# Six banks for the first row maxima, and the expert biases fetched tile by tile: one change in a two-layer attention and mixture-of-experts kernel

## What is computed

```python
h = jax.nn.silu(xs @ Wg[e] + bg[e]) * (xs @ W1[e] + b1[e])
out = out + we[:, e:e + 1] * (h @ W2[e] + b2[e])
```

## Time and profile before

| | us |
|---|---|
| median of three runs | 2758.1 |
| lowest and highest of the three | 2752.99 and 2760.24 |
| the profiled execution, its own time | 2755.3 |
| its span, first to last instruction | 2753.6 |
| TensorE busy in it | 2312.6 (84%) |
| ScalarE busy | 1497.1 (54%) |
| VectorE busy | 1156.7 (42%) |
| GpSimd busy | 387.3 (14%) |

### The profile page before, as it was taken

The page is one execution under the profiler, slowest core; times in us unless marked ns, Lnnn a source line. Parts: engine busy times, 40 slices in busy tenths (PEclk is TensorE's granted clock), DMA queues, the critical chain, the costliest instruction groups (busy, mean ns, idle before and its releaser), DMA issues. The chain is left out here.

```text
span 2753.6 us, 40775 instructions
## 1 busy us (share of the span) xinstructions
PE 2312.6 (84%) x13037; PEld 1080.1 (39%) x13038; DVE 1156.7 (42%) x2545; ACT 1497.1 (54%) x2463; POOL 387.3 (14%) x632
## 2 busy tenths in 40 slices
PE   5995899807949999999999999997258999999993
PEld 3783555404611222222222222223125666666662
DVE  5566322275854444444444444422464222222223
ACT  2213333234718999999999999995643222222220
POOL 0020466520000000000000000000001222222220
PEclk9997999958959999999999999998679999999996
DMA  4001122252000000000000000002351000000004
GB/s 170 1 1 62 51 76 78 67 203 90 29 0 1 1 1 1 1 1 1 1 1 1 1 1 1 1 1 82 104 169 37 31 30 30 30 30 30 30 27 193
DMA packets 50002, 114.78 MB, mean 42 GB/s; under 512 B 7368, under 2 KB 25424, under 8 KB 49872
## 3 DMA queue, kind: packets, MB, share of 16 engines
q1 hardware_dynamic: 35088, 71.63, 7.8%
q0 software_dynamic: 13632, 37.24, 4.2%
q10 hardware_dynamic: 1152, 4.19, 0.4%
HBM read 73.46 MB, written 39.58 MB: 41 GB/s over the span
## 5 line engine op out<-in xcount | busy, mean ns | idle before, releaser
L1641 ACT ACTIVATE at_pexp<-at_psS 128x1024 f32<-128x1024 f32 x1024 | 972.4, 1023 | 144.3 <-PE at_psS L1556 132.6
L1655 DVE TENSOR_REDUCE at_mx<-at_psM 128x1 f32<-128x512 f32 x512 | 353.8, 691 | 558.2 <-PE at_psM L1583 558.0
L1570 PE MATMUL at_psO<-at_pexp,at_vst 128*32 128x512 f32 x4096 | 547.1, 606 | 0.4 <-ACT at_pexp L1641 0.4
L1556 PE MATMUL at_psS<-l1c_QT,l1c_KT 64*128 64x512 f16 x2048 | 466.6, 385 | 53.2 <-ACT at_pexp L1641 39.9
L1993 PE MATMUL ex_psH<-wide_wgu,ex_xT 128*128 x852 | 362.2, 548 | 0.0
L1583 PE MATMUL at_psM<-at_ksumT,l1c_QT 64*128 64x512 bf16 x512 | 206.7, 404 | 33.8 <-DVE at_mx L1655 29.3
L2037 ACT ACTIVATE ex_sg<-ex_psH 128x228 f32<-128x228 f32 x213 | 77.0, 361 | 287.0 <-PE ex_psH L1993 287.0
L1583 PEld LDWEIGHTS at_psM<-at_ksumT,l1c_QT 64*128 64x128 f16 x512 | 47.7, 93 | 451.3 <-issue 245.8
L2060 DVE TENSOR_TENSOR ex_h<-ex_psH,ex_sg 128x228 f32<-128x228 f32 x213 | 84.3, 396 | 317.9 <-ACT ex_sg L2037 317.9
L1556 PEld LDWEIGHTS at_psS<-l1c_QT,l1c_KT 64*128 64x128 f16 x2048 | 97.5, 93 | 294.9 <-ACT at_pexp L1641 285.3
L1993 PEld LDWEIGHTS ex_psH<-wide_wgu,ex_xT 128*128 128x128 f32 x852 | 162.3, 191 | 124.9 <-issue 123.2
(11 more groups left out here) (340 smaller groups left out, 2669.9 us busy)
## 6 DMA issues: line engine op xcount, KB each, us to landing
normed<-rt_area SPq DMA_DIRECT2D x16, 512.0 KB, 2.7
lm_y<-expert_rows SPq DMA_DIRECT2D x16, 512.0 KB
cb_y<-expert_rows SPq DMA_DIRECT2D x16, 512.0 KB, 9.9
w_raw<-in_L_ffn_w SPq DMA_DIRECT2D x24, 256.0 KB, 4.3
wide_wgu<-in_L_ffn_Wg SPq DMA_DIRECT2D x8, 684.0 KB
wide_wgu<-in_L_ffn_W SPq DMA_DIRECT2D x8, 684.0 KB
wide_w2b<-in_L_ffn_W SPq DMA_DIRECT2D x8, 684.0 KB
res_x<-in_L_attn_x SPq DMA_DIRECT2D x8, 512.0 KB
```

What stands on the lines that cost most here:

```text
L1556: mm = pe.matmul(psS[:, n, hh * BANK:(hh + 1) * BANK], keys(k.KT, p)[r, kt * P:(kt + 1) * P], keys(k.QT, p)[r, c * BANK:(c + 1) * BANK], s ...
L1570: mm = pe.matmul(psO[g * VW:(g + 1) * VW, y, :], vst[:, p % 2, hh, kt, :], pexp[:, y * 2 + n, hh * BANK:(hh + 1) * BANK], start=(kt == 0), ...
L1641: act.activation(pexp[:, u % 4, :], psS[:, u % 2, :], ACT.Exp, scale=D ** -0.5 / (QS * QS)).then_inc(raised, 1)
L1655: dve.tensor_reduce(mx[:, n:n + 1], psM[:, :], AX.X, ALU.max).then_inc(reduced, 1)
```

## The change

- In `attention`, the products of pair 0 and the first six of pair 1 go by twos (both heads of a query tile) into one of three pairs of banks, the four of `psS` and the two of `psO` (`early`), and VectorE reduces both in one instruction. The sum of the keys of pair 1 is made after the second reduction, and the six maxima of pair 1 come ahead of the copies of the shift. TensorE waits for all 38 maxima before the loop.
- The stage `prepare_biases` goes, with its tables and the bias products on TensorE.
- In `experts1`, SyncE loads for every tile the two bias rows of its expert, each spread over all 128 partitions, into a ring of two. VectorE adds them to the products (out of PSUM, into the ring's place in SBUF). ScalarE and the multiplication of VectorE read from there. A bank of `psH` is free when the addition is done (`added`).

The diff, cut to its core:

```diff
+        def early(at):
+            return (psS[:, 0, :], psS[:, 1, :], psO[:, :, :].rearrange("p a c -> p (a c)"))[at % 3].rearrange(
+                "p (h c) -> p h c", h=2)
...
+                def first_means(p, t):
+                    at = p * KT16 + t
+                    if t == 0:
+                        pe.wait_ge(k_ready, p + 1)
+                    if at >= 3:
+                        pe.wait_ge(reduced, 2 * (at - 3) + 2)
+                    for hh in range(2):
+                        r = slice(hh * HR, (hh + 1) * HR)
+                        pe.matmul(early(at)[:, hh, :], keys(k.QT, p)[r, t * P:(t + 1) * P], ksumT[r, p % 2, :],
+                                  start=True, stop=True).then_inc(maxed, 1)
...
-                for n in range(ST):
-                    means(0, n)
+                for t in range(KT16):
+                    first_means(0, t)
+                for t in range(AHEAD // 2):
+                    first_means(1, t)
                 for half in range(2):
                     turn_shift(0, half)
-                for n in range(AHEAD):
-                    means(1, n)
+
+                pe.wait_ge(reduced, ST + AHEAD)
...
+                def first_reduce(p, t):
+                    at = p * KT16 + t
+                    dve.wait_ge(maxed, 2 * at + 2)
+                    dve.tensor_reduce(mx[:, 2 * t:2 * t + 2], early(at), AX.X, ALU.max).then_inc(reduced, 2)
...
                 sum_keys(0)
-                for n in range(ST):
-                    reduce(0, n)
+                for t in range(KT16):
+                    if t == 2:
+                        sum_keys(1)
+                    first_reduce(0, t)
                 make_shift(0)
-                sum_keys(1)
+                for t in range(AHEAD // 2):
+                    first_reduce(1, t)
                 put_shift(0, 0)
                 put_shift(0, 1)
-                for n in range(AHEAD):
-                    reduce(1, n)
...
+        BR = 2
+        bias = s.sb("bias", [P, BR, HG, 2, HW])
...
+            @block.sync
+            def _(sp):
+                for st in steps(sp, NTILE, 4, 0):
+                    t, r = st.tile(0), st.slot(0, BR)
+                    e = sp.value_load(k.tile_expert[0:1, ds(t, 1)], min_val=0, max_val=E - 1)
+
+                    st.again(sp, h_done, (t - BR + 1) * HG)
+                    for n, w in enumerate(("L1_ffn_bg", "L1_ffn_b1")):
+                        sp.dma_start(bias[:, r, :, n, :], a[w][ds(e, 1), :].rearrange(
+                            "a (g c) -> (a g) c", g=HG).partition_broadcast(P)).then_inc(bias_in[r], 16)
...
-                            st.again(pe, h_done, t * HG - HG + n + 1)
-                            pe.matmul(psH[:, n, 0:G2], k.pick[:, ds(e, 1), :].rearrange("p a c -> p (a c)"),
-                                      k.bias[:, n * G2:(n + 1) * G2], start=True, stop=False)
+                            st.again(pe, added, t * HG - HG + n + 1)
...
-                                                   "p a n c -> p (a n) c"), start=False, stop=(kk == KC - 1))
+                                                   "p a n c -> p (a n) c"), start=(kk == 0), stop=(kk == KC - 1))
...
-                            act.wait_ge(h_ready, t * HG + n + 1)
+                            act.wait_ge(added, t * HG + n + 1)
...
-                            act.activation(sg[:, n, :], psH[:, n, 0:HW], ACT.Silu).then_inc(gated, 1)
+                            act.activation(sg[:, n, :], bias[:, st.slot(1, BR), n, 0, :], ACT.Silu).then_inc(gated, 1)
...
-                        for n in range(HG):
-                            dve.wait_ge(gated, t * HG + n + 1)
-                            dve.tensor_tensor(h[:, j, n, :], psH[:, n, HW:2 * HW], sg[:, n, :],
-                                              ALU.mult).then_inc(h_done, 1)
+                        dve.wait_ge(bias_in[st.slot(0, BR)], st.lap(0, BR) * 32 + 32)
+                        for n in range(HG + 1):
+                            if n < HG:
+                                dve.wait_ge(h_ready, t * HG + n + 1)
+                                hb = bias[:, st.slot(0, BR), n, :, :]
+                                dve.tensor_tensor(hb, psH[:, n, 0:G2].rearrange("p (n c) -> p n c", n=2), hb,
+                                                  ALU.add).then_inc(added, 1)
+                            if n:
+                                m = n - 1
+                                dve.wait_ge(gated, t * HG + m + 1)
+                                dve.tensor_tensor(h[:, j, m, :], bias[:, st.slot(0, BR), m, 1, :], sg[:, m, :],
+                                                  ALU.mult).then_inc(h_done, 1)
...
-            k.bias = wide.sb("bias", [P, HG * 2 * HW], BF16, side="right")
-            k.pick = wide.sb("pick", [P, E, P], BF16, side="right")
-            prepare_biases(nc, k, a)
```

More of the change, by code:

```diff
@@ L1892, in load_experts, with experts1 @@
         sp.dma_start(k.w2b[HP:HP + 1, e, HK - 1, :], a["L1_ffn_b2"][e:e + 1, :]).then_inc(k.w_in[e], 16)
[L1895 to L1938, removed]
+def experts1(nc, k, a):
     G2 = 2 * HW
@@ L1955, in experts1 @@
         (x_turned, x_out, h_ready, gated, h_done, h_turned, hl_out, hr_out, y_ready,
-         y_done, start) = (
+         y_done, start, added) = (
             s.sem(v) for v in ("xturned", "xout", "hready", "gated", "hdone", "hturned", "hlout", "hrout", "yready",
-                               "ydone", "start"))
+                               "ydone", "start", "added"))
+        bias_in = s.sems("biasin", BR)
         got, put = s.sems("got", GR), s.sems("put", 2)
@@ L2149, in program @@
             k.w_in = wide.sems("win", E)
-            k.bias = wide.sb("bias", [P, HG * 2 * HW], BF16, side="right")
-            k.pick = wide.sb("pick", [P, E, P], BF16, side="right")
-            prepare_biases(nc, k, a)
             attention_out(nc, k, lambda sp: load_experts(sp, k, a, range(E // 2)))
         route(nc, k, "rt1", 1, k.cent, k.x, lambda sp: load_experts(sp, k, a, range(E // 2, E)))
-        experts1(nc, k)
+        experts1(nc, k, a)
         combine(nc, k, "cb1", out.rearrange("b (p t) c -> p b t c", p=P))
```

## The result

The changed kernel takes **2677.96 us** (median of 4 runs, 2677.37 to 2679.49), against 2757.44 us for the kernel before (4 runs, three of them those of the first table, 2752.99 to 2760.24). The ratio is 0.9715, with a 95% interval of 0.9703 to 0.9727: 79.5 us less. The forecast was 2676 us. The profiled execution took 2679.49 us with a span of 2677.6 us, against 2753.6 us before.

The account below looks back on a forecast made before the run. Bounds: ScalarE in the attention loop, TensorE in the experts, TensorE and VectorE taking turns in the first maxima. Savings 25.8 + 14.5 + 1.5 + 40.5 = 82.3 us from 2755.3, plus 2.8 to the median: 2676 us, range 2665 to 2704.

Parts of the forecast that it names:

- Expert steps: Experts of layer 1: without bias products a step falls from 8.64 to 8.07 us, 40.5 us less in all.
- Bias stage: Between attention and its output: the removed stage no longer holds TensorE up, 14.5 us less.
- First maxima: Attention, first reduction to first scores: VectorE becomes the bound, 32.1 us instead of 57.9, 25.8 less (22 to 29).
- The tail: End of the first maxima: second shift copy starts 3.05 us after the first, takes 1.4, then 0.1 to the scores.
- Clock: Start of the attention's output: TensorE stands still 2 us instead of 16; 1.5 us less, bounds 0 and 2.
- The first bias: Start of the experts: first tile's bias, issued with the first gather, costs 0 to 3 us once, taken as 0.
- The bias transfer: Experts, each tile: 700 KB of bias loads take 6.5 us (3.5 to 9.6), hidden with 1 or 2 us to spare.
- Both rivals of the stream: Experts: bias loads half bind, 2676 to 2716 us, chance 0.09; or set the pace, 2841 us, chance 0.07.
- The clock rival: Before the attention loop: denser TensorE work raises its clock early, saving up to 3 us, 2673 us; chance 0.08.
- The lower end of the range: Whole kernel: 2665 us, from the bounds of the head and start (-5, -3) and a run's scatter.

Follow-up runs that it names:

- The doubled product: The kernel before with the bias product issued a second time in each group: 2796.53 us, ratio 1.0154.
- bias_after_rows: The changed kernel with the bias loads of tiles 0 and 1 issued only after that tile's rows are gathered and transposed: 2670.92 us, ratio 0.9694.
- bias_stream_more: The changed kernel with 10 broadcast bias pieces a partition and tile instead of 6, the extra ones unread: 2677.98 us, ratio 0.9719.

## Why the prediction was right, step by step

**Expert steps: right.** 40.5 us forecast, 40.1 measured over the whole stretch; the step 8.07 forecast, 8.06 measured. The doubled product showed the price by itself, 0.196 us each. VectorE has 238.89 of 500 us, 3.85 us a step, where 4.0 was expected, and TensorE is never idle for it.

**Bias stage: right.** 14.5 forecast, 14.7 measured.

**First maxima: right in kind, 2.8 us too small.** The terms that were mis-sized are those of the reductions. The forecast took 1.26 us from one to the next; the stretch from 774.38 to 794.80 holds 16 of them and one `sum_keys` of 2.28 us, so (20.42 - 2.28) / 16 = 1.13 us, 2.1 us less. The three of pair 1 with `make_shift` took 799.06 - 794.80 = 4.26 us instead of 4.55. The length of 1.22 us was right; what failed is the distance to the next one, which lies 0.09 us under the length where the forecast put 0.04 us on top. The last term is the 0.43 for the second product of the first pair, taken as one product after the other: a pair takes 0.61 us, as a single product did, and the first reduction starts 0.73 us after the start of its products instead of 0.62. The tail, 3.05 us between the copies and 1.51 to the scores, is as forecast. The bounds stated for this place, 22 to 29 us, don't follow from their own terms: 19 reductions at 1.04 and 1.38 us give 30.0 and 23.5. Either way the 28.6 lies inside.

**Clock: the step failed.** "I take 1.5 us" for the start of the attention's output came to nothing; that stretch is 0.2 us longer. TensorE stood still for 1.64 us instead of 16.31, and yet the granted clock was 1.00 up to 1864.8 and 0.59 in the 4.2 us after. The 0.56 of the earlier trace rows is for a window that starts 0.13 us ahead of the work; over the same 4.17 us from the first transpose the kernel before shows 0.60. Eight transposes took 1.72 us instead of 1.94, the first eight products 3.02 instead of 2.76, and the ninth transpose starts 4.41 us after the first instead of 4.38: the shorter pause brought nothing. Ahead of it TensorE had worked for only 0.63 of the 2.8 us from 1862.0. What the clock follows here was not tried.

**The first bias: the step failed.** "0 to 3 us once, taken as 0" asked when the bias itself would land, and by itself a late bias costs nothing, as `bias_after_rows` shows. What was not asked is what the loads do to the transfer issued beside them. The first gather, on which TensorE waits, is issued 0.09 us after the first of loads with 1.4 MB, and 5.6 us came of it in this execution (4.5 to 5.6 in the kernels with the same loads). It was outside the bounds given for that term, and the underrated gain of the first maxima covered half of it.

**The bias transfer: within its bounds, but taken too slow.** 6.5 us were taken for the data, and the changed kernel shows 4.2. In the steady step shown the loads issued at 2254.57 are through before 2260, and the addition that needs them starts at 2265.98, so 6 us were to spare where the prediction counted 1 or 2. The fit of the Trainium skill (DMA: Bandwidth & Descriptors, Anatomy of one DMA), which the page gives for transfers issued by GpSimd while these are SyncE's, gave an estimate of 3.6 us with its fixed part. The data alone took longer than that from one row, and 2.6 us from distinct rows. Both rivals of the stream fall: it did not set the pace, and even 1.67 times the pieces left the step at 8.06 us. The clock rival did not come: the granted clock is 0.50 from 789 to 804 us, up to the first scores, and the loop behind them shows at most 0.8 us of the 3.

Together: -28.6 - 14.7 - 40.1 - 0.8 + 5.6 + 0.2 - 0.4 is -78.8, and with the +2.8 of scatter it is the -76.0 between the profiles. The forecast of -82.3 was 3.5 us off the sum without scatter. That it was so near is in part luck: two errors of opposite sign, 2.8 and 5.6 us, partly cancel, and neither was foreseen. The lower end of the range took 5 and 3 us for bounds that its own terms put at 4.2 and 0.5; the measured time is far from that end.

## What to carry to other kernels

When a load is added beside others at the start of a stage, ask not only when it lands but which transfer issued in the same moment has someone waiting for it; hold the new load until that one is in, and look whether the engine can run ahead meanwhile. Here one wait on SyncE brought some 5 us. A short product in a dense chain costs the distance from its start to the next start, not its duration. Two engines that take turns over one buffer gain from the second buffer; a third one brought nothing once the slower engine was full.

## What the runs showed of the hardware that was not expected

- Two products with 64 rows each, on rows 0 to 63 and 64 to 127 and into different banks, take 0.61 us together at a granted clock of 0.50 to 0.54, where one takes 0.61. The Trainium skill has the rule (TensorEngine Tiling (Array Packing), Key Properties): different tiles can load weights and multiply in parallel. The trace agrees.
- Copies of one row come slower from memory than distinct rows: 0.70 MB in 4.2 us against 2.6 us.
- A gather on GpSimd's queue is delayed by loads on SyncE's: at the start of the experts gathers land in 5.3 to 8.2 us, in the steady steps in 2.8. The steady steps do not bring the two together, though: the loads of the step shown are through when its gather is issued at 2259.76. In `bias_stream_more` they still run then, and the gathers land in 3.0 to 4.0 us. The Trainium skill (DMA: Bandwidth & Descriptors, Queues, rings and completion order) says that each engine goes round its queues packet by packet. If every turn moves as many bytes, a gather of 0.13 MB is held up by about as many bytes of the loads, an estimate of 0.8 us at the 162 GB/s of that stretch. With distinct rows the first transpose comes 0.9 us late, near that; with copies of one row it is 4.5 to 5.6 us. So for copies of one row the trace does not agree with that rule alone, and why the delay is longer stays open. The view of the first 5 gathers:

```profile
L999 POOL DMA_INDIRECT ex_xg<-normed,ex_idx x5: 956/958/1025, 2046.6 to 2056.9; - x5
...
DMA to landing us min/median/max: 5.3/6.9/8.2
```

- Reductions of 1024 columns in a row are 1.22 us long but 1.13 us apart (four in 4.61 us, above).
- A silu of 228 columns takes 393 ns from SBUF, where from PSUM it took 0.36 us.
